# A Mamba, quantised-expert and mixture-of-experts layer on one core: the last part of the gap between two scans reordered, and the expert stage started three units earlier

## What is computed

```python
x = x + mamba(layernorm(x))          # per batch
x = x + quant_mlp(layernorm(x))      # two int8-like linears with scales from column and row maxima
x = x + moe(layernorm(x))            # 16 experts, top 2, and one shared expert

def mamba(h):                        # DI = 1024 channels, DS = 16 states
    x, z = in_proj(h)
    u = silu(conv4(x))
    dt, B, C = split(x_proj(u))
    delta = softplus(dt_proj(dt) + bias)
    h_t = h_{t-1} * exp(delta_t * A) + (delta_t * u_t) * B_t     # one scan over 512 tokens
    y_t = sum_n h_t[n] * C_t[n] + u_t * D
    return out_proj(y * silu(z))
```

## Time and profile before

| what | value |
|---|---|
| runs | 1648.01 us median of 3 (1646.08 to 1650.48) |
| profiled execution | 1643.62 us, its span 1641.9 us |
| TensorE busy | 1420.1 us (86%) |
| VectorE busy | 1338.5 us (82%) |
| GpSimd busy | 1038.7 us (63%) |
| ScalarE busy | 800.9 us (49%) |
| exp(delta A) on ScalarE | 512 times, 690 ns |
| scan on VectorE | 432 + 64 times, 1219 and 1211 ns |
| product on VectorE | 240 + 192 times, 671 and 669 ns |
| chunk on GpSimd | 255 times, 2373 ns |

### The profile page before, as it was taken

The page is one execution under the profiler, slowest core; times in us unless marked ns, Lnnn a source line. Parts: engine busy times, 40 slices in busy tenths (PEclk is TensorE's granted clock), DMA queues, the critical chain, the costliest instruction groups (busy, mean ns, idle before and its releaser), DMA issues.

```text
span 1641.9 us, 19427 instructions
## 1 busy us (share of the span) xinstructions
PE 1420.1 (86%) x5462; PEld 833.4 (51%) x5462; DVE 1338.5 (82%) x2196; ACT 800.9 (49%) x1365; POOL 1038.7 (63%) x672
## 2 busy tenths in 40 slices
PE   7588679998799899998799899998799999647994
PEld 4333234444665565444665565444665664335783
DVE  4588999687999999797999999797999999773212
ACT  3675454257544755247545755347545664131131
POOL 0399899104999898404999898404999898322002
PEclk9799889999799999999799999999799999868997
DMA  3550000413447673614447783614446773601984
GB/s 122 226 192 26 1 0 15 159 46 137 166 148 223 213 243 98 217 39 163 167 147 229 211 240 103 210 39 171 165 146 200 219 240 105 226 26 52 347 326 140
DMA packets 94074, 252.14 MB, mean 154 GB/s; under 512 B 11024, under 2 KB 11152, under 8 KB 88848
## 3 DMA queue, kind: packets, MB, share of 16 engines
q1 hardware_dynamic: 86688, 229.93, 41.7%
q0 software_dynamic: 5120, 16.78, 3.1%
q10 hardware_dynamic: 2160, 4.19, 0.7%
HBM read 207.87 MB, written 42.99 MB: 153 GB/s over the span
## 4 chain that ended last, share of the span: by engine, by line
PE 50%; DVE 23%; issue 12%; ACT 6%; POOL 6%; DMA 2%; DVEq 0%; POOLq 0%; SPq 0%; ACTq 0%
PE bank L1993 12%; DVE bank L1308 6%; PE bank L1835 5%; PE bank L2119 5%; PE bank L1925 4%; PE bank L1930 4%; PE bank L2022 3%; PE bank L1919 3%; POOL work L688 3%; PE bank L2014 2%; PE bank L1848 2%; PE bank L1969 2%; PE bank L1937 2%; DVE work L1318 2%; DVE pairs L1318 2%
## 5 line engine op out<-in xcount | busy, mean ns | idle before, releaser
L688 POOL TENSOR_TENSOR work<-du,BB 128x1024 f32<-128x1024 f32 x255 | 602.3, 2373 | 5.1 <-DVE work L1579 3.5
L980 ACT ACTIVATE bank<-delta,A_sb 128x512 f32<-128x512 f32 x512 | 349.4, 690 | 433.1 <-DVE pairs L1318 241.6
L1308 DVE TENSOR_TENSOR_SCAN bank<-bank,work 128x512 f32<-128x512 f32 x432 | 522.6, 1219 | 7.9 <-ACT bank L980 6.0
L1993 PEld LDWEIGHTS bank<-x3T,ew_up 128*128 128x128 f32 x1488 | 220.3, 195 | 70.5 <-issue 59.4
L1993 PE MATMUL bank<-x3T,ew_up 128*128 128x128 f32 (+1 forms) x1488 | 242.3, 309 | 2.2 <-issue 2.2
L1318 DVE TENSOR_TENSOR pairs<-bank,CB 128x512 f32<-128x512 f32 x240 | 161.0, 671 | 3.4 <-PE bank L1930 2.9
L1925 PE MATMUL bank<-pairs,ident 128*128 128x512 f32 x160 | 91.6, 657 | 43.5 <-POOL pairs L741 16.9
L1318 DVE TENSOR_TENSOR work<-bank,CB 128x512 f32<-128x512 f32 x192 | 128.4, 669 | 0.0
L640 POOL TENSOR_TENSOR col<-col,halfpow 128x4 f32<-128x4 f32 (+1 forms) x8 | 7.8, 974 | 176.0 <-DVE col L1456 176.0
L2119 PE MATMUL bank<-wst,zg 128*128 128x512 f32 x256 | 117.0, 593 | 0.8 <-DVE zg L1328 0.8
L1848 PE MATMUL bank<-xT,wst 128*128 128x512 f32 x256 | 115.6, 596 | 0.0
(11 more groups left out here) (261 smaller groups left out, 2438.4 us busy)
## 6 DMA issues: line engine op xcount, KB each, us to landing
ew_up<-in_exp_w SPq DMA_DIRECT2D x93, 512.0 KB
ew_dn<-in_exp_w SPq DMA_DIRECT2D x93, 256.0 KB, 4.3
hm<-xs_dram SPq DMA_DIRECT2D x69, 256.0 KB, 4.6
ys_dram<-x3T SPq DMA_DIRECT2D x69, 256.0 KB, 4.6
wst<-in_w_in SPq DMA_DIRECT2D x64, 256.0 KB, 2.7
BB<-bc_dram SPq DMA_DIRECT2D x16, 1024.0 KB, 4.9
CB<-bc_dram SPq DMA_DIRECT2D x16, 1024.0 KB, 7.0
wst<-in_out_w SPq DMA_DIRECT2D x32, 256.0 KB, 2.7
```

The source lines that it names most:

```text
L688: nc.gpsimd.tensor_tensor(dBu[:, k % CHUNK_SLOTS, :, :], du[:, j % 2:j % 2 + 1, :].broadcast_to([P, 2, T]), BB[:, n0:n0 + 2, :], ALU.mult) ...
L980: nc.scalar.activation(R[q % RING][:, :], delta[:, j, :], ACT.Exp, scale=A_sb[:, j, n:n + 1]).then_inc(S["da_ready"], 1)
L1308: V.tensor_tensor_scan(prod[c % (2 * PAIR_SLOTS)] if on_pool(q) else R[q % RING][:, :], R[q % RING][:, :], dBu[:, c // 2 % CHUNK_SLOTS, c ...
L1993: ins = mm(gu_bank(v)[:, part * n:(part + 1) * n], w[:, part * D + k * P:part * D + (k + 1) * P], rhs, start=(k == 0), stop=(k == KD - 1))
```

## The change

Three things change, all in order and none in what is computed.

1. The tables `STAGE` (not `LATE`), `HEAD_AT` and `OUT_AT`: visits, heads and out_proj parts stand 3 units earlier, routing 2, logits 1. `HEAD_AT` and `OUT_AT` hold for the scan of batch 0 as well.
2. The gap's end: ScalarE computes relu and exp of blocks 4 to 7 earlier and normalises rows before the last z copy and before the first three `decay`; TensorE issues `dl(5)` and `dl(6)` (the dt projections) earlier; GpSimd does `norm` before the delta operations of blocks 2 and 3.
3. VectorE's `one_more` and `lost` of blocks 4 to 7 leave the gap and stand behind scans 0 and 1; ScalarE's logarithms of these blocks stand behind its x3T copies.

```diff
--- before.py
+++ after.py
@@ -80,8 +80,8 @@
     first_down: int
 
 
-STAGE = Order(visits=tuple(4 + 4 * v for v in range(SHARED)) + tuple(38 + 3 * r for r in range(ROUTED)),
-              x3=0, logits=1, route=5, rank=9, place=10, first_down=12)
+STAGE = Order(visits=tuple(1 + 4 * v for v in range(SHARED)) + tuple(35 + 3 * r for r in range(ROUTED)),
+              x3=0, logits=0, route=3, rank=7, place=8, first_down=10)
 LATE = Order(visits=tuple(4 + 4 * v for v in range(SHARED)) + tuple(38 + 3 * r for r in range(ROUTED)),
              x3=0, logits=2, route=5, rank=9, place=10, first_down=12)
 RAW_Z = 2
@@ -117,9 +117,9 @@
 EARLY_LOST_AT = {1: 6, 2: 7, 3: 8, 4: 29, 5: 30, 6: 31, 7: 32}
 EARLY_SUM_AT = {1: 5, 2: 6, 3: 6, 4: 18, 5: 19, 6: 20, 7: 21}
 EARLY_LESS_AT = {1: 7, 2: 8, 3: 9, 4: 21, 5: 22, 6: 23, 7: 24}
-HEAD_AT = (103, 105, 107, 109)
-OUT_AT = ((114, 107, 111, 116), (114, 108, 112, 117), (115, 109, 112, 118), (116, 110, 113, 118),
-          (119, 120, 120, 121), (122, 122, 123, 124), (124, 125, 126, 126))
+HEAD_AT = (100, 102, 104, 106)
+OUT_AT = ((111, 104, 108, 113), (111, 105, 109, 114), (112, 106, 109, 115), (113, 107, 110, 115),
+          (116, 117, 117, 118), (119, 119, 120, 121), (121, 122, 123, 123))
 
 
 def on_pool(q):
@@ -721,12 +721,12 @@
                         softplus_less(a, i)
                     du_block(a, 0)
                     chunk(a, 0)
-                    for i in range(2, 4):
-                        softplus_sum(a, i)
-                        softplus_less(a, i)
-                if m is not None:
-                    norm(2 * m + 1)
+                    softplus_sum(a, 2)
+                norm(2 * m + 1)
                 if a is not None:
+                    softplus_less(a, 2)
+                    softplus_sum(a, 3)
+                    softplus_less(a, 3)
                     chunk(a, 1)
 
             def scan_stage(b, scan, experts):
@@ -1049,6 +1049,8 @@
                         if p == at.x3:
                             for i in range(KD if scan else KD // 2):
                                 x3(i)
+                            if scan:
+                                lns(b, range(4, 8))
                     if scan and b > 0:
                         for m in SILU_AT.get(p, ()):
                             z_silu(b, m)
@@ -1186,17 +1188,16 @@
                 weight_scales(m, 1)
                 exps(a, range(3, 4))
                 lns(a, range(4))
-                relus(a, range(4, 5))
+                relus(a, range(4, 7))
+                exps(a, range(4, 7))
                 z(a, 5)
-                relus(a, range(5, 6))
+                relus(a, range(7, 8))
+                exps(a, range(7, 8))
                 z(a, 6)
-                relus(a, range(6, 8))
-                exps(a, range(4, 8))
+                row_norm(m, 2 * m + 1)
                 z(a, 7)
                 for c in range(RING):
                     decay(a, c)
-                row_norm(m, 2 * m + 1)
-                lns(a, range(4, 8))
 
             def last(m):
 
@@ -1378,6 +1379,10 @@
                 for p in range(UNITS + TAIL):
                     if scan and p < UNITS:
                         scan_unit(p)
+                    if scan and b > 0 and p < 2:
+                        for i in (4 + 2 * p, 5 + 2 * p):
+                            one_more(b, i)
+                            lost(b, i)
                     if scan and b == 0:
                         for i in range(1, NBLK):
                             if p == EARLY_LOST_AT[i]:
@@ -1636,10 +1641,6 @@
                 q1.transposed(1)
                 second_residual(m, q1)
                 row_stats(m, 2 * m + 1)
-                for i in range(4, 8):
-                    one_more(a, i)
-                    lost(a, i)
-
             def last(m):
 
                 q0, q1 = Quant(m, 0), Quant(m, 1)
@@ -2186,12 +2187,12 @@
                 integers(m, 1, 0)
                 integers(m, 1, 1)
                 dl(a, 4)
+                dl(a, 5)
                 linear(m, 1)
+                dl(a, 6)
                 z(a, 5)
-                dl(a, 5)
+                dl(a, 7)
                 z(a, 6)
-                dl(a, 6)
-                dl(a, 7)
                 z(a, 7)
 
             def last(m):
```

## The result

The changed kernel took 1662.74 us (median of 7 runs, 1658.31 to 1667.20), the kernel before 1648.53 beside it (7 runs, 1645.29 to 1653.90): ratio 1.0086, 95% interval 1.0072 to 1.0100. It is 0.86% slower, where 1645.1 within 1633 to 1653 was forecast. Lines of kernel.py have moved by one to five: `nsum` is L1920/1926/1931, `rank` L1947 to L1951, `gated` L1329, the transposes of routed rows L1970.

The account below looks back on a forecast made before the run. TensorE was taken to pace each scan's first quarter, by a hair, and its end, VectorE the middle; 1.3 + 2 x (3.5 - 2.1) + (0.9 - 2.1) = 2.9 us saved gave 1645.1 us, range 1633 to 1653.

Parts of the forecast that it names:

- the middle: Middle of each scan: routed visits keep their pattern against the sums and VectorE sets the pace as now; 0.
- The gap: Between two scans: first scan starts 11.7 us earlier, but scan 3 stays where it is; 0, bounds 2.3 earlier, 1.6 later.
- First quarter: Start of each scan: TensorE idles before `rank`, slow clock behind it, `gated` of block 1 later; -2.1 us per scan.
- End of scans 1 and 2: TensorE's last `down` and block 7 end earlier, shortening VectorE's wait of 6.46; +3.5 us each, bounds 2.5 to 4.6.
- End of scan 3: Last scan's chain ends otherwise, so only the wait of 1.47 at `gated` of block 6 shortens; +0.9 us.
- Scan 0: First scan: two head transposes fill idle time and the clock stays up longer; +1.3 us, bounds 0.9 to 2.8.
- C: Rival: slower, the slow clock behind `rank` lasts 12.6 us, loss above 4 per scan; 1654, up to 1658; chance 0.16.
- D: Rival: no change, the tail is bound elsewhere and front and end cancel; 1648 us; chance 0.14.
- B: Rival: the gap's gain holds, TensorE keeps its clock or `lost` collides less; 1629 to 1638 us; chance 0.25.

Follow-up runs that it names:

- s7: Changed kernel with GpSimd's gate weights at pair 15 instead of 17; 1646.66 us, ratio to before 0.9995.
- s12: Kernel before with one edit, the gate weights at pair 15 instead of 17; 1646.38 us, ratio to before 0.9987.
- s2: Changed kernel's gap alone, with the tables of the kernel before; 1645.84 us, ratio to before 0.9991.
- s15: s13 with routed visits, head transposes and output projection back where the kernel before has them; 1646.57 us, ratio to before 0.9987.
- s13: s7 with the router's steps one unit earlier, at unit 2 instead of 3; 1638.08 us, ratio to before 0.9941.
- s14: s7 with the router's steps two units earlier, at unit 1 instead of 3; 1638.82 us, ratio to before 0.9943.
- s16: s14 with GpSimd's scatters of routed rows one pair earlier as well; 1635.73 us, ratio to before 0.9920.
- s9: Changed kernel's gap and end, first quarter of before, routed visits 4, 7 and 10 one unit closer; 1645.83 us, ratio to before 0.9993.
- s4: Changed kernel with routed visits, head transposes and output projection where the kernel before has them; 1654.28 us, ratio to before 1.0043.
- s1: Changed kernel with GpSimd's scatters of routed rows one pair earlier; 1659.47 us, ratio to before 1.0072.

## Why the prediction was wrong

The step that failed is **the middle**: "Routed visits stand 3 units earlier with a pitch of 3 units, so their pattern against the sums is the same with each visit one ahead. [...] The term is 0." The visits keep their pattern against the sums, but not against GpSimd and SyncE. I looked for the cover of the shared weights (visit 2) and not for that of the first routed rows; a view of the waits of the weight-load queue in the third scan would have shown it, 0.8 us with the name of the DMA beside it. What the runs put in its place: 4.3 to 5.0 us of wait and up to 2.8 of slow clock behind it in each scan, 15 to 16 us in all (1662.7 against 1646.7 in s7, which differs in the gate weights' place alone). s12 makes the same edit where there is no such wait, and gains nothing that can be told.

s7 is the kernel that the prediction described but for this wait, of which 3.2 us are left, and the other steps can be read there. Its ratio of 0.9995 (0.9981 to 1.0009) leaves room for the 2.9 us forecast and for nothing at all:

- **The gap, 0.** Right. The first scan of the second gap starts 102.2 us behind the last `gated`, against 113.3 before: 11.1 earlier (11.4 and 10.7 in the other two gaps), 11.7 forecast. Scan 3 comes 0.7, 0.4 and 0.0 sooner in the three, where 0 stood. `lost` beside chunks takes 2.72. s2 shows the whole of it: no measurable gain.
- **First quarter, -2.1 per scan.** Right: `gated` of block 1 comes 1.1, 2.2 and 2.1 later than before. The slow clock behind `rank` is there (0.50 from 812.50 to 819.49 in the changed kernel), and so are the waits of 2.2 at `places` and 2.0 at `gated` of block 0 too. What the prediction cites from the Trainium skill against the change held, and what it costs was in the sum.
- **End of scans 1 and 2, +3.5.** Right: wait 6.46 to 3.02, blocks 2 to 7 3.6 and 3.7 shorter in s7, and s15, which undoes it together with the end of scan 3 and of scan 0, loses 8.5 us by medians.
- **End of scan 3, +0.9.** Right in kind. Blocks 2 to 7 gain 4.3 there in s7, and VectorE's wait for the gathered rows grows from 4.56 to 8.24 behind them: 0.6 is left.
- **Scan 0, +1.3.** Too high, it is 0: 247.9 us from its first scaled row to its end, before and in the changed kernel. The wait of block 7 fell from 8.17 to 4.74, and that of block 6 rose from 2.01 to 4.36, behind the output matmuls that now stand ahead of its sum. Nor was the idle 2.62 filled: TensorE idles 2.94 there in the changed kernel and 4.64 in s7, now for ScalarE's copy of the next batch's head.
- **Rivals.** C has the right sign by the wrong mechanism: it put the loss behind `rank`, at most at 1658, and it lay in block 1, with 1662.7 measured. D and B are out: the end moved, and the clock was lost.

Not settled is why s13 gains 8.6 us of median on s7 (8.9 by the ratios; they ran on different chips) where the profiles have 5.8. That TensorE kept its clock behind the shorter idle time is not what the profiles show: over the 10 us from the start of `rank` it was granted 0.57, 0.50 and 0.60 in s7 and 0.58, 0.55 and 0.52 in s13.

## What to carry to other kernels

When work is moved earlier on one engine, list every input that it takes, with the time at which it is there and the time at which it is now wanted; the ones without slack show as waits of a few tenths on a queue that looks unimportant. A load released by two events is only as early as the later one, so moving the obvious one may show nothing. And look at what shares the buffer: here two tiny operations, in the way for no reason but storage, decided between 0.9% slower and no change. With the router's steps one unit earlier besides, the kernel was 0.6% faster than before.

## What the runs showed of the hardware

- Behind the wait of 4.95 us TensorE ran 6.69 us at 0.58 of its clock: 2.8 us lost (0.42 of 6.69), more than half of the wait itself again.
- The length of the idle time does not decide alone. In the third scan of s14 the clock was 1.00 from 794 to 799, TensorE idled 1.93 ahead of `rank`, and from 801 to 809 it was granted 0.50: the sums (L1920, L1926) took 2.06 and 1.91 instead of 1.02. In s16 it was 1.30 of idle time, with 0.50 from 801 to 807. But in s9 it idled 3.07 ahead of 916.36 and was granted 1.00 behind it, and in s4 1.91 and 1.73 between 917 and 932, at 1.00 throughout. What tells the cases apart is open. The windows of s14, then of s9:

```profile
794.00:799.00 5.00, 4.31 (x20) 3.44 (x19) 4.91 (x19) 2.74 (x6) 4.56 (x4) 1.00 0.50 210
801.00:809.00 8.00, 8.00 (x26) 5.93 (x26) 7.83 (x17) 2.99 (x5) 8.00 (x7) 0.50 0.49 197
```

```profile
916.40:921.00 4.60, 4.60 (x20) 2.85 (x21) 4.60 (x6) 3.04 (x6) 4.60 (x3) 1.00 0.57 182
```

- A small VectorE operation can be held up for long beside GpSimd. The scale step of the next batch's norm (128x4, two SBUF inputs) took 7.23 us in one scan of s4, and 7.22 in one of s1. GpSimd ran without a break over all of it in both, and had its first idle time, of 1.33, as it ended. In the same scan of the kernel before it takes 0.17. The scans concerned are 6.6 and 6.9 us longer behind block 1, which fits that the profiled executions of s4 and s1 lie above their medians (1659.94 and 1663.66):

```profile
928.93 7.23 DVE L1262 SCALAR_TENSOR_TENSOR shift<-mv,rstd 128x4 f32<-128x4 f32 x1
```

- SyncE issues the row load 0.41 behind the start of the gate weights where these release it (before, after, s1), and 2.7 behind the start of the last scatter where that does (s7): the load waits until the scatter's data have landed.
